# Local attention in a 16-head block loop: scores and values issued in two halves, k ahead of q, and the floor of the norms taken by a reduction over pairs

## The reference, cut to what matters

```
def attn_layer(x, Wqkv, qs, ksc, Wo):
    q, k, v = split(x @ Wqkv)                  # 16 heads of 64 each
    q = l2norm(q) * qs ; k = l2norm(k) * ksc   # t / max(norm(t), 1e-12)
    q = q*cos*scale + rotate_half(q)*sin*scale
    k = k*cos/scale + rotate_half(k)*sin/scale
    # window w looks at the keys of windows w-1 and w
    sim = einsum('bhwie,bhwje->bhwij', q, look(k)) * 8.0, masked
    out = einsum('bhwij,bhwje->bhwie', softmax(sim), look(v))
    return out @ Wo
def ffn_layer(x, g, bln, W1, b1, W2, b2):
    xn = layernorm(x) * g + bln
    a, gate = split(xn @ W1 + b1)
    return a * gelu(gate) @ W2 + b2
```

## Time and profile before

| | |
|---|---|
| Time, median of 3 runs | 4685.8 us (4681.85 to 4686.91) |
| Profiled execution, its own time | 4681.54 us |
| Its span | 4679.7 us |
| Busy: TensorE (PE), VectorE (DVE), ScalarE (ACT), GpSimd (POOL) | 3977.7, 3228.5, 2529.5, 1193.6 us |
| Mean granted TensorE clock, of full speed | 0.914 |

### The profile page before, as it was taken

How to read it: one execution, slowest core, us unless ns; L and a number is a source line. 1 busy time by engine, 2 the same in 40 slices (tenths; PEclk the granted TensorE clock), 3 DMA queues, 4 the chain that set the end, 5 groups by cost and what they waited for, 6 DMA issues and landing times.

```text
span 4679.7 us, 114797 instructions
## 1 busy us (share of the span) xinstructions
PE 3977.7 (85%) x46878; PEld 2233.9 (48%) x46974; DVE 3228.5 (69%) x5280; ACT 2529.5 (54%) x3698; POOL 1193.6 (26%) x1015
## 2 busy tenths in 40 slices
PE   3688888888888888866668999999998499999997
PEld 1355555555555555534434555555554133333333
DVE  7688878888888788854432665656664577667772
ACT  4356666666666565652122555555553266666665
POOL 0255556555556555500000000000000011111110
PEclk7899999999999999965567999999999699999999
DMA  0122222222222222200000000000000301110000
GB/s 17 65 59 77 62 61 73 67 58 78 61 71 65 60 81 61 60 15 17 19 13 16 3 2 4 4 4 3 4 1 6 114 2 24 21 26 17 19 2 14
DMA packets 84462, 166.49 MB, mean 36 GB/s; under 512 B 22472, under 2 KB 36472, under 8 KB 82704
## 3 DMA queue, kind: packets, MB, share of 16 engines
q1 hardware_dynamic: 83952, 159.13, 13.0%
HBM read 40.60 MB, written 8.52 MB: 10 GB/s over the span
## 4 chain that ended last, share of the span: by engine, by line
PE 63%; DVE 13%; issue 11%; ACT 8%; DMA 2%; SPq 2%; POOL 1%; DVEq 0%; POOLq 0%; ACTq 0%
PE banks L503 6%; PE banks L1238 5%; PE banks L2178 5%; PE banks L1209 4%; PE banks L1221 4%; PE banks L582 4%; PE banks L598 3%; PE banks L544 3%; PE banks L618 2%; PE banks L561 2%; ACT arena L2316 2%; PE banks L2152 2%; PE banks L535 2%; ACT arena L710 2%; PE banks L2136 2%
## 5 line engine op out<-in xcount | busy, mean ns | idle before, releaser
L2390 DVE TENSOR_REDUCE arena<-banks 128x2 f32<-128x1024 f32 x512 | 614.0, 1222 | 277.9 <-PE banks L2143 141.8
L2316 ACT ACTIVATE arena<-banks 128x1024 f32<-128x1024 f32 x512 | 522.8, 1025 | 282.7 <-PE banks L2159 147.2
L939 POOL TENSOR_TENSOR arena<-arena 128x512 f32<-128x512 f32 x384 | 425.4, 1129 | 755.1 <-DVE arena L824 747.5
L943 POOL TENSOR_TENSOR arena<-arena 128x1024 f32<-128x1024 f32 x192 | 533.0, 2776 | 15.1
L1391 DVE CUSTOM_DVE_ANT_0 arena<-arena,banks 128x512 f32<-128x512 f32 (+3 forms) x640 | 361.6, 602 | 235.2 <-issue 233.9
L1334 ACT ACTIVATE arena<-banks 128x512 f32<-128x512 f32 (+3 forms) x320 | 170.1, 532 | 418.9 <-PE banks L1221 418.2
L503 PE MATMUL banks<-arena 128*128 128x512 f32 x768 | 355.6, 607 | 31.4 <-ACT arena L673 24.4
L2178 PE MATMUL banks<-arena 128*32 128x256 f32 x4096 | 334.5, 393 | 17.2 <-issue 11.6
L1326 ACT ACTIVATE arena<-arena 128x128 f32<-128x128 f32 (+15 forms) x256 | 328.5, 1285 | 11.2 <-DVE arena L1403 6.3
L1209 PE MATMUL banks<-arena 64*128 64x512 f32 (+3 forms) x1280 | 326.1, 582 | 9.2 <-issue 8.0
L1221 PEld LDWEIGHTS banks<-consts,arena 128*128 128x128 f32 x2176 | 233.1, 141 | 189.6 <-DVE arena L1410 102.4
(11 more groups left out here) (432 smaller groups left out, 7618.2 us busy)
## 6 DMA issues: line engine op xcount, KB each, us to landing
arena<-arena SPq DMA_DIRECT2D x768, 64.0 KB
arena<-arena SPq DMA_DIRECT2D x96, 384.0 KB, 3.6
arena<-arena SPq DMA_DIRECT2D x96, 128.0 KB, 3.4
arena<-in_lf_wqkv SPq DMA_DIRECT2D x6, 1024.0 KB, 5.3
arena<-features_k SPq DMA_DIRECT2D x32, 128.0 KB
arena<-arena SPq DMA_DIRECT2D x8, 512.0 KB
arena<-features_q SPq DMA_DIRECT2D x16, 216.0 KB
arena<-in_lf_wqkv SPq DMA_DIRECT2D x6, 512.0 KB, 3.8
```

The lines of the kernel that those rows point to most:

```text
L939: nc.gpsimd.tensor_tensor(r[:, :, e * H2:(e + 1) * H2], q[:, j, :, (1 - e) * H2:(2 - e) * H2], s[:, j, 1, e * H2:(e + 1) * H2].unsqueeze(1 ...
L943: nc.gpsimd.tensor_tensor(a, a, lf_rb, ALU.add).then_inc(S("lf_rot" + x), 1)
L2316: nc.scalar.activation(bi_PT[n % 4], PS[:, 2 * bi_slot("S", n):2 * bi_slot("S", n) + 2].rearrange("p a b -> p (a b)"), ACT.Exp).then_inc(S ...
L2390: nc.vector.tensor_reduce(bi_max[j % 2][:, t, :, c], PS[:, 2 * slot:2 * slot + 2], AX.X, ALU.max).then_inc(S("bi_mx"), 1)
```

## The change

1. `qk` computes k (banks 2 and 3) first and q (banks 0 and 1) second. `lf_qn` is awaited by every block; `lf_ot` (the copy of the values out of banks 0 and 1) only ahead of q. `squares` and `norm` take k first too.
2. `scores` is issued in two halves of four column groups, `turn_q` between them. `lf_s` is raised at the end of the second half.
3. `turn_k` stands right behind `vv`, ahead of the wait for `lf_v` and the feed-forward products.
4. `values_ready` stands between the two products of `up`; in phase 0 it stands between `down` and `mean`.
5. `values` is issued in two halves, `project` between them. `lf_pv` is raised at the end of the second half.
6. The floor of the norms was a `tensor_scalar` maximum over 32 values. The sums now go to every second place of a buffer whose other places hold 1e-24, and a `tensor_reduce` maximum over the pairs writes 32 values to a buffer of their own.
7. SyncE's load of the next layer's q and k weights waits for `lf_q`, now the later of the two.

```diff
--- before.py
+++ after.py
@@ -366,7 +366,8 @@
         lf_mask = arena.bf16(2 * CH).rearrange("p (a b) -> p a b", a=2)
         lf_xb = arena.f32_3(4, P)
         lf_sqb = z_xc
-        lf_n2 = arena.f32(2 * HEADS)
+        lf_n2 = arena.f32_3(2 * HEADS, 2)
+        lf_n2m = arena.f32(2 * HEADS)
         lf_ri = arena.f32(2 * HEADS)
         lf_qn = z_sq
         lf_rb = ck(z_std, 0, INNER)
@@ -466,7 +467,7 @@
                 if more and s in (NB - 1, NB, NB + 3, NB + 8):
                     following = bass.ds(l + 1, 1)
                 if more and s == NB - 1:
-                    sp.wait_ge(S("lf_k"), l * NB + NB)
+                    sp.wait_ge(S("lf_q"), l * NB + NB)
                     lf_load_qk(sp, following)
                     sp.wait_ge(S("lf_tb"), l * NB + NB)
                     lf_load_scales(sp, following)
@@ -495,11 +496,13 @@
                 if n % NB == 0:
                     pe.wait_ge(S("lf_wqk_in"), (l + n // NB) * 16 + 16)
                 pe.wait_ge(S("lf_xb"), l * 2 * NB + (2 * n + 2))
-                if n >= 4:
-                    pe.wait_ge(S("lf_ot"), l * NB + (n - 3))
-                elif n >= 1:
-                    pe.wait_ge(S("lf_qn"), n)
-                for j in range(4):
+                if n >= 1:
+                    pe.wait_ge(S("lf_qn"), l * NB + n)
+                for j in (2, 3, 0, 1):
+                    if j == 0:
+
+                        if n >= 4:
+                            pe.wait_ge(S("lf_ot"), l * NB + (n - 3))
                     m = nc.tensor.matmul(PS[:, j], lf_xb[:, n % 4], ck(lf_wqk, j), start=True, stop=True)
                     if j % 2:
                         m.then_inc(S("lf_q" if j == 1 else "lf_k"), 1)
@@ -544,23 +547,25 @@
                     m = nc.tensor.matmul(PS[:, 6 + j], lf_xb[:, n % 4], ck(lf_wv, j), start=True, stop=True)
                 m.then_inc(S("lf_vmm"), 1)
 
-            def scores(n, l, end):
-
-                pe.wait_ge(S("lf_kT"), l * NB + (n + 1))
-                if n >= 3:
-                    pe.wait_ge(S("lf_y2"), l * NB + (n - 2))
-                c, j, ffn = lf_chunk(n + 1, end)
-                if ffn and j == 0:
-                    pe.wait_ge(S("lf_lnv"), l * NCH + (c + 1))
-                for b in range(2):
-                    nc.tensor.matmul(PS[:, 4 + b], lf_irep, lf_mask[:, 0 if n % NB == 0 else 1], start=True, stop=False, skip_group_check=True)
-                for p in range(8):
+            def scores(n, l, end, half):
+
+                if half == 0:
+                    pe.wait_ge(S("lf_kT"), l * NB + (n + 1))
+                    if n >= 3:
+                        pe.wait_ge(S("lf_y2"), l * NB + (n - 2))
+                    c, j, ffn = lf_chunk(n + 1, end)
+                    if ffn and j == 0:
+                        pe.wait_ge(S("lf_lnv"), l * NCH + (c + 1))
+                    for b in range(2):
+                        nc.tensor.matmul(PS[:, 4 + b], lf_irep, lf_mask[:, 0 if n % NB == 0 else 1], start=True, stop=False, skip_group_check=True)
+                for p in range(4 * half, 4 * half + 4):
                     for h in range(2):
                         r = slice(DH * h, DH * (h + 1))
                         for w in range(4):
                             m = nc.tensor.matmul(PS[WIN * w:WIN * (w + 1), 4 + h, p * DH:(p + 1) * DH], lf_qT[r, p, WIN * w:WIN * (w + 1)],
                                                  lf_kT[n % 2][r, p, WIN * w:WIN * w + 2 * WIN], start=False, stop=True, skip_group_check=True)
-                m.then_inc(S("lf_s"), 1)
+                if half:
+                    m.then_inc(S("lf_s"), 1)
 
             def values_ready(n, l, end):
 
@@ -571,17 +576,18 @@
                 pe.wait_ge(S(f"lf_vs{n % 2}"), l * 16 * NB + (32 * (n // 2) + 32))
                 pe.wait_ge(S(f"lf_z{n % 2}"), l * 64 * NB + (128 * (n // 2) + 128))
 
-            def values(n, l):
-
-                for e, vb in ((0, lf_Vs[n % 4]), (1, lf_V[n % 4])):
-                    for p in range(8):
-                        for a in range(2):
-                            for h in range(2):
-                                r = slice(DH * a, DH * (a + 1))
-                                hd = 2 * p + h
-                                m = nc.tensor.matmul(PS[DH * h:DH * (h + 1), a, (2 * p + e) * WIN:(2 * p + e + 1) * WIN], vb[r, hd * DH:(hd + 1) * DH],
-                                                     lf_Z[r, e * HEADS + h * 8 + p], start=True, stop=True, skip_group_check=True)
-                m.then_inc(S("lf_pv"), 1)
+            def values(n, l, e):
+
+                vb = (lf_Vs if e == 0 else lf_V)[n % 4]
+                for p in range(8):
+                    for a in range(2):
+                        for h in range(2):
+                            r = slice(DH * a, DH * (a + 1))
+                            hd = 2 * p + h
+                            m = nc.tensor.matmul(PS[DH * h:DH * (h + 1), a, (2 * p + e) * WIN:(2 * p + e + 1) * WIN], vb[r, hd * DH:(hd + 1) * DH],
+                                                 lf_Z[r, e * HEADS + h * 8 + p], start=True, stop=True, skip_group_check=True)
+                if e:
+                    m.then_inc(S("lf_pv"), 1)
 
             def project(n, l, end):
 
@@ -630,10 +636,14 @@
                 if lf_live(s, end):
                     qk(s, l)
                 if lf_live(s - 2, end):
-                    scores(s - 2, l, end)
+                    scores(s - 2, l, end, 0)
                 if lf_live(s - 1, end):
                     turn_q(s - 1, l, end)
+                if lf_live(s - 2, end):
+                    scores(s - 2, l, end, 1)
+                if lf_live(s - 1, end):
                     vv(s - 1, l)
+                    turn_k(s - 1, l)
 
                     if ffn or ending:
                         pe.wait_ge(S("lf_v"), l * NB + s)
@@ -643,17 +653,19 @@
                     down(b, l)
                 if ffn and j:
                     up(c, j - 1, l, 0)
+
+                if lf_live(s - 3, end):
+                    values_ready(s - 3, l, end)
+                if ffn and j:
                     up(c, j - 1, l, 1)
                 elif ffn:
                     mean(c, l)
                 if lf_live(s - 3, end):
-                    values_ready(s - 3, l, end)
-                if lf_live(s - 1, end):
-                    turn_k(s - 1, l)
-                if lf_live(s - 3, end):
-                    values(s - 3, l)
+                    values(s - 3, l, 0)
                 if lf_live(s - 4, end):
                     project(s - 4, l, end)
+                if lf_live(s - 3, end):
+                    values(s - 3, l, 1)
                 if ffn and j == 0:
                     var(c, l)
 
@@ -673,7 +685,7 @@
                 nc.scalar.activation(lf_xb[DH:P, n % 4], lf_y[DH:P, t * P:(t + 1) * P], ACT.Copy).then_inc(S("lf_xb"), 1)
 
             def squares(n, l):
-                for j, x in enumerate("qk"):
+                for j, x in ((1, "k"), (0, "q")):
                     act.wait_ge(S("lf_" + x), l * NB + (n + 1))
                     if n >= 1:
                         act.wait_ge(S("lf_red" + x), l * NB + n)
@@ -683,7 +695,7 @@
                 act.wait_ge(S("lf_n2"), l * NB + (n + 1))
                 if n >= 1:
                     act.wait_ge(S("lf_qn"), l * NB + n)
-                nc.scalar.activation(lf_ri, lf_n2, ACT.Ln, scale=float(2 ** RL2)).then_inc(S("lf_ln"), 1)
+                nc.scalar.activation(lf_ri, lf_n2m, ACT.Ln, scale=float(2 ** RL2)).then_inc(S("lf_ln"), 1)
                 act.wait_ge(S("lf_ln"), l * NB + (n + 1))
                 nc.scalar.activation(lf_ri, lf_ri, ACT.Exp, scale=-0.5, bias=lf_one[:, 1:2]).then_inc(S("lf_rinv"), 1)
 
@@ -793,20 +805,22 @@
             dve.wait_ge(S("lf_const_in"), 16 * 4)
             st(nc.vector.tensor_copy(lf_irep, lf_const[:, 0:P]))
             st(nc.vector.tensor_copy(lf_mask.rearrange("p a b -> p (a b)"), lf_const[:, P:P + 2 * CH]))
+            st(nc.vector.memset(lf_n2[:, :, 1:2], 1e-24))
             nc.vector.memset(lf_y2[:, 0:1], 0.0).then_inc(S("lf_zeroed"), 1)
             for c in range(NCH):
                 nc.vector.tensor_copy(ck(lf_y[:, 1:T + 1], c), ck(xn, c)).then_inc(S("lf_y"), 1)
             dve.wait_ge(S("lf_zeroed"), 1)
 
             def norm(n, l):
-                for j, x in enumerate("qk"):
+                for j, x in ((1, "k"), (0, "q")):
                     dve.wait_ge(S("lf_sq" + x), l * NB + (n + 1))
-                    if j == 0 and n >= 1:
-                        dve.wait_ge(S("lf_ln"), l * NB + n)
-                    nc.vector.tensor_reduce(ck(lf_n2, j, HEADS), ck(lf_sqb, j, INNER).rearrange("p (a b) -> p a b", b=DH), AX.X, ALU.add).then_inc(S("lf_red" + x), 1)
+                    nc.vector.tensor_reduce(lf_n2[:, j * HEADS:(j + 1) * HEADS, 0], ck(lf_sqb, j, INNER).rearrange("p (a b) -> p a b", b=DH), AX.X, ALU.add).then_inc(S("lf_red" + x), 1)
                 dve.wait_ge(S("lf_redq"), l * NB + (n + 1))
```

(5 more changed lines are left out.)

## The result

| | before | after |
|---|---|---|
| Time, median | 4684.9 us (4 runs) | 4740.4 us (4 runs, 4732.77 to 4741.67) |
| Ratio | 1 | 1.0116, 95% interval 1.0098 to 1.0133 |
| Span of the profiled execution | 4679.7 us | 4739.0 us |

The account below looks back on a forecast made before the run. TensorE and VectorE, busy 1556 and 1540 of 1823 us, were both near their limits. Four steps sum to +2.2, over 24 chunks +53; spells +10, "issue" waits -6: +57, 4738.5, adjusted to 4740; 8-in-10 range 4655 to 4805.

Parts of the forecast that it names:

- ScalarE's run behind the values: From `keep_o` on: ends at T+3.7 (T: start of `qk`), second square T+5.7 against T+4.7, 1.0 us of delay.
- k ahead of q: In `qk`: the new wait for `lf_ot` is covered by k's 1.8 us; taken as 0.
- The scores' halves: Around `turn_q`: `keep_q` still waits for the scores' end, no gain; 0, bounds 0.25 us won and 0.5 lost.
- The floor: On VectorE between sum and maximum: 0.25 us against a median of 0.73, so 0.5 us less.
- `turn_k` and the wait inside `up`: Phases 2 and 3: wait for `scale` ends T+12.2, step closes T+17.1, 0.15 us more each, 0.3 together.
- Phase 0: Late squares, later values and an exposed 1.75 us wait ahead of `var`: +3.05 us a step, T to T 22.2.
- the slow spells: TensorE at 1.2 GHz behind idle times, 1.6 us each: six spells, 10 us; bounds none and 77 us.
- Phase 1: VectorE is the path: `scale` ends T+11.65, the step T+16.85 against 18.0 before, 1.15 us less.
- Rival A: Faster: VectorE alone sets the pace, longer waits are slack; 51 us less, 4633; chance 0.20.
- B: Much slower: TensorE at 1.2 GHz behind most waits of phase 0; 67 us more, 4807; 0.12 with the table-load case.
- C: No change: the waits for v that go (117 us) pay for phase 0's 73 us; about 4685; chance 0.13.
- The rule weighed for the table load: ScalarE: 2.66 us switch would make squares 2.4 us late instead of 1.0, some 67 us more, 4807; 0.12 with B.

## Why the prediction was right, point by point

**ScalarE's run behind the values.** Forecast: `block_in` ends at T+3.7, second square at T+5.7. Measured T+3.71 and T+5.67. The experiment with the load ahead takes 1.3 us out of this run and gives back 59 us: the longer way behind the values' end is most of the cost. It is not all: with the load ahead in both, the halves of values and scores still cost 38 us (4681.3 against 4642.9). `keep_o` still starts with the next `qk` there, and the wait of 1.67 ahead of `var` is still in every phase 0.

**k ahead of q.** Taken as 0. It was never run alone, so that stays open; the run with values and scores whole leaves little room for it.

**The scores' halves.** Forecast 0, with no `vv` before T+7.2 and T+7.65 behind a load; measured T+7.64. Right in the reason too, by the experiment with the load ahead. The second half ended at T+6.9 and not at the T+6.5 of the forecast, and the load that ends at T+6.97 just hid this, which is luck: without the load `vv` could not start before T+7.6 either.

**The floor.** Its length was nearly right, 0.25 forecast and 0.22 measured:

```profile
L823 DVE TENSOR_REDUCE arena<-arena x96: 220/221/224, 186.8 to 2000.8; 128x32 f32<-128x64 f32 x96
```

What it is worth was wrong. I took 0.5 us off VectorE's path wherever it closes a step; in the changed kernel it is worth 3.5 us in all, or nothing. I carried the old floor's median of 0.73 into an order in which the same instruction takes 375 ns in the mean. The rule weighed there from the Trainium skill ("SBUF — State Buffer", Who interferes with whom), that `tensor_scalar` can be held by the port pair which GpSimd shares and `tensor_reduce` cannot, agrees with the trace: 182 to 1689 ns against 220 to 224, though a GpSimd instruction was running as 64 of these 96 reductions started. How much of the excess remains when the instruction moves is settled by where GpSimd's instructions then lie.

**`turn_k` and the wait inside `up`.** Forecast: second product at T+12.2, step closed at T+17.1. Measured T+12.20 and 17.20 to 17.34. Against the mean of the phases before, 17.28 and 18.11, this is no loss but 4 us of gain over all. The 16.95 was the mean of two chosen steps, too low: before, phases 2 and 3 held 21 us of waits marked "issue", and after they hold none. That term was +7, or +1 with the 6 us that the sum took off for such waits, and came out as -4.

**Phase 0.** Forecast +3.05 a step; measured +4.01, 88 us over 22 steps instead of 67. `vv` at T+8.94 (forecast T+8.95), the wait ahead of `var` 1.67 (1.75; the working took 0.55 for the `square`, whose row has 0.62). The shortest steps but the first, without a spell, take 22.5, near the 22.2 forecast. The mis-sized term is the slow spells. Over one-microsecond windows with a granted clock below 0.95, each busy time weighted by how far the clock had fallen, TensorE worked for what is 39 us at half clock between 310 and 1960 before, and 102 us between 310 and 2000 after. Half of that time is lost, so 31 us more than before, where I had put 10. Some 20 of it lie in phase 0 by an estimate from its steps, 515 us against 22 times 22.5.

**Phase 1.** Forecast -1.15 a step, -25 for 22; measured -26, and in part by luck. The new step was right, 16.85 against a median of 16.98, but the one taken for before, 18.0, was short: the 17 steps that do not begin a layer's feed-forward part had a mean of 18.75 and gain 1.65 each, 28 us, and the five that do lose 2. The forecast also contains 0.5 for the floor, which the run with the old floor does not bear out in this size (phase 1 took 430.2 with it and 423.5 without, 0.3 a step).

**Left out.** Steps 1 to 7 gain 13 us, with no gate and no load behind the values. Some 8 of these are the clock, by an estimate: counted as above, the work at half clock from 177 to 310 us went from 37 to 22 us. The tail loses 11 us. Neither was in the sum, and that they nearly cancel is luck.

The sum was +57 and the span grew by 59, closer than its terms: phase 0 with its spells was 11 us too low (88 against 67 and 10), and phases 2 and 3 were 11 too high. The mechanism is borne out; that the time came within 1 us of 4740 is luck. Rival A is refuted: VectorE's busy time did fall and the kernel got slower. Of B, part is true: more slow spells, 31 us from 310 us on and not 77. C is refuted by the time, and in the trace by `scale`, which ends the wait inside `up` in phases 2 and 3, where C needed it not to be last. The rule weighed for the table load, a switch of 2.66 us ("ScalarE: Activation LUTs", What ACT_TABLE_LOAD costs, in the Trainium skill), is not seen in any row: the load starts at 1207.20, and the gelu and `block_in` behind it are over by 1209.72. In all 72 steps with a gate the gelu starts 1.30 us behind the start of its load, before and after.

## What to carry to other kernels

When a stage is cut in two to fill a gap, its end moves later, and everything that waits for the end moves with it: list what stands in the queues behind that waiter, through table loads and copies, before counting the gap. Raising the semaphore at the end of the second half while the consumer needs all of it means that the first half's early finish serves nobody. An edit's worth belongs to the order it was measured in: the same floor was worth 25 us in one order and nothing that could be told in the other, and moving the load of the gelu gave 59 us beside the halves and nothing without them; so test parts on both kernels.

## What the runs showed of the hardware

A `tensor_scalar` over 32 columns took 182 to 185 ns where no GpSimd instruction was running as it started, and otherwise could last until 35 to 46 ns behind the end of that instruction, 1689 ns at most before and 2370 in the changed order. Its mean was 780, 375 and (in the kernel before with k first and halved values) 223 ns. A `tensor_reduce` over 64 columns in its place took 220 to 224 ns in all 96 cases of the changed kernel. Behind waits of 2.0 to 2.2 us `vv` ran slow in 6 of the 22 phases 0 of the changed kernel, in 3 with `shifted` behind the squares and in 15 with `square` ahead of `keep_o`, and then mostly cost 1.1 to 1.7 us more; behind the waits of 0.7 to 0.9 us of the run with the gelu's load ahead it never did. Waits marked "issue" on TensorE, 17.5 us ahead of the values before, are near 0 after the change without one instruction less. Where the new order waits for a semaphore close ahead, they no longer show; what they wait for was not tested.
